# Flamingo-style stack of eight gated layers on one core: the last batch's attention result stays in an SBUF tile

## The reference

```
# layer 0: 16 heads of 32, a second small attention over the last 16 context rows is added
ctx = _attn(q, k, v) + _attn(q, k_dca, v_dca)
x = x + tanh(g_xattn[0]) * (ctx @ Wo + bo)
...
# layer 3: 32 heads of 16, rotary positions
attn = einsum('bhqk,bhkd->bqhd', softmax(q k^T * scale), v)
x = x + tanh(g_xattn[3]) * (attn @ Wout + bout)
# behind it: a mixture of experts, 2 shared and 16 routed, top 2, on _layernorm(x)
```

## Time and profile before

| | us |
|---|---|
| median of 3 runs | 3114.33 (3113.45 to 3116.43) |
| the profiled execution, its own time | 3107.09 |
| its span in the trace | 3105.4 |
| TensorE busy in the span | 2389.4 |
| VectorE busy | 2056.9 |
| ScalarE busy | 1503.2 |
| GpSimd busy | 1075.3 |
| mean granted TensorE clock | 0.906 of full |

### The profile page before, as it was taken

The page is one execution under the profiler, slowest core; times in us unless marked ns, Lnnn a source line. Parts: engine busy times, 40 slices in busy tenths (PEclk is TensorE's granted clock), DMA queues, the critical chain, the costliest instruction groups (busy, mean ns, idle before and its releaser), DMA issues. The chain is left out here.

```text
span 3105.4 us, 39908 instructions
## 1 busy us (share of the span) xinstructions
PE 2389.4 (77%) x13100; PEld 1074.2 (35%) x13100; DVE 2056.9 (66%) x3302; ACT 1503.2 (48%) x2076; POOL 1075.3 (35%) x818
## 2 busy tenths in 40 slices
PE   2989997899969934676666489928898888796882
PEld 0542332344434311222222256614422222353551
DVE  6658774545456798999997652246588888456523
ACT  2554554254332765555553353325557777433642
POOL 4766765011001235666664121155541000001224
PEclk9998999899979967889987599968889999998996
DMA  4542221120000000000000462254522100313735
GB/s 157 179 171 86 86 86 66 63 86 1 1 4 13 1 0 1 0 1 0 0 0 28 136 200 86 82 152 155 209 96 82 61 9 15 103 48 130 247 129 194
DMA packets 128413, 245.60 MB, mean 79 GB/s; under 512 B 32515, under 2 KB 59407, under 8 KB 126310
## 3 DMA queue, kind: packets, MB, share of 16 engines
q1 hardware_dynamic: 107094, 169.49, 15.6%
q0 software_dynamic: 21136, 73.68, 7.7%
HBM read 154.24 MB, written 88.60 MB: 78 GB/s over the span
## 5 line engine op out<-in xcount | busy, mean ns | idle before, releaser
L1901 DVE TENSOR_REDUCE ac_nmax<-ac_M 128x1 f32<-128x512 f32 (+1 forms) x768 | 491.6, 677 | 75.4 <-PE ac_M L1734 70.8
L1883 ACT ACTIVATE ac_PT<-ac_S 128x1024 f32<-128x1024 f32 x384 | 388.0, 1021 | 187.4 <-PE ac_S L1761 168.4
L3477 POOL TENSOR_TENSOR sc_hc<-sc_h,sc_cs 128x1024 f32<-128x1024 f32 x128 | 300.5, 2355 | 157.2 <-DVE sc_h L3592 93.0
L3592 DVE TENSOR_TENSOR_SCAN sc_h<-sc_dA,sc_dB 128x1024 f32<-128x1024 f32 x128 | 292.1, 2282 | 12.3 <-ACT sc_dA L3558 12.3
L3512 PE MATMUL sc_y<-sc_hc,ident 128*128 128x512 f32 x512 | 258.0, 631 | 18.6 <-DVE x_res L3608 16.3
L3558 ACT ACTIVATE sc_dA<-ss_delta,sc_A 128x511 f32<-128x511 f32 x256 | 166.0, 682 | 28.8 <-DVE sc_h L3592 28.0
L774 DVE SCALAR_TENSOR_TENSOR mo_y16l<-mo_yT,mo_y16h 128x512 f16<-128x512 f32 x86 | 59.4, 690 | 180.6 <-ACT mo_y16h L717 180.4
L3490 PE MATMUL sc_b<-ss_bc,sc_sel 128*128 128x512 f16 x128 | 53.5, 418 | 154.1 <-DVE sc_dB L3584 122.7
L3584 DVE TENSOR_TENSOR sc_dB<-ss_du,sc_b 128x1024 f32<-128x1024 f32 x128 | 156.1, 1220 | 17.7 <-PE sc_b L3490 6.9
L3563 ACT ACTIVATE sc_cs<-sc_c 128x512 f32<-128x512 f32 x128 | 76.2, 596 | 185.3 <-POOL sc_hc L3477 182.3
L1734 PE MATMUL ac_M<-KT,QT 64*128 64x512 f16 (+1 forms) x384 | 135.7, 428 | 31.9 <-DVE ac_nmax L1901 17.3
(11 more groups left out here) (622 smaller groups left out, 5716.1 us busy)
## 6 DMA issues: line engine op xcount, KB each, us to landing
keys_t<-ap_kto SPq DMA_DIRECT2D x32, 512.0 KB, 2.6
queries_t<-ap_qto SPq DMA_DIRECT2D x32, 512.0 KB, 2.7
slot_results_last<-mo_o SPq DMA_DIRECT2D x47, 256.0 KB
slot_results<-mo_o SPq DMA_DIRECT2D x39, 256.0 KB
values<-ap_vf SPq DMA_DIRECT2D x32, 256.0 KB, 2.9
ac_KT<-keys_t POOLq DMA_DIRECT2D x4, 2048.0 KB, 8.8
ac_QT<-queries_t POOLq DMA_DIRECT2D x16, 512.0 KB, 10.4
attended<-ac_A SPq DMA_DIRECT2D x8, 1024.0 KB, 3.8
```

The lines of the kernel that those rows point to most:

```text
L1883: nc.scalar.activation(PT[:, n % PTB, :, :], psS[:, 2 * (n % 2):2 * (n % 2) + 2, :], ACT.Exp, scale=SCALE / (SQK * SQK)).then_inc(exp_done, 1)
L1901: last = v.tensor_reduce(out[:, :, 0], sc[:, 0:MAIN], AX.X, ALU.max)
L3477: nc.gpsimd.tensor_tensor(hc[:, m % RC, :, :], h[:, m % RH, :, :], cs[:, m % 2, :].unsqueeze(1).to_broadcast([P, W, S]), ALU.mult).then_in ...
L3592: nc.vector.tensor_tensor_scan(h[:, m % RH, :, :].rearrange("p c s -> p (c s)"), dA[:, m % 2, :, :].rearrange("p c s -> p (c s)"), dB[:, m ...
```

## The change

In both attention layers the last batch's result is written into `Vc` in place of `A`, it is neither stored nor loaded, and the blocks behind the core take the row tiles in the order 12, 13, 14, 15, 0, 1, ..., 11. `Vc` now lives until the end of the layer, where it was freed with the core's tiles. In `attention_output_block` the tile `A` holds three batches. The wait of VectorE for the third batch's store goes too, since the fourth batch has a tile of its own.

```diff
@@ attention_core_block
+        def attended(b):
+            return w["Vc"] if b == B - 1 else A
...
-            sp.wait_ge(whole, B * NG)
-            sp.dma_start(w["a_d"][B - 1], A[:]).then_inc(a_out, 16)
-            sp.wait_ge(a_out, 16 * B)
+            sp.wait_ge(a_out, 16 * (B - 1))
...
-                av = A[:, :, c0:c0 + GH * HD].rearrange("p j (h d) -> p j h d", d=HD)
+                av = attended(G // NG)[:, :, c0:c0 + GH * HD].rearrange("p j (h d) -> p j h d", d=HD)
...
-                if g % NG == 0 and b and i == 0:
+                if g % NG == 0 and 0 < b < B - 1 and i == 0:
                     dve.wait_ge(a_out, 16 * b)
...
@@ attention_output_block
-        A = sb("A", [P, B, TPB, D])
+        A = sb("A", [P, B - 1, TPB, D])
...
+        def attended(t):
+            return w["Vc"][:, t, :] if t < TPB else A[:, t // TPB - 1, t % TPB, :]
+
+        def row_tile(t):
+            return (t + NT - TPB) % NT
...
-            for b in range(B):
+            for b in range(B - 1):
                 sp.dma_start(A[:, b], w["a_d"][b]).then_inc(a_in[b], 16)
...
-                if t % TPB == 0:
-                    pe.wait_ge(a_in[t // TPB], 16)
+                if t and t % TPB == 0:
+                    pe.wait_ge(a_in[t // TPB - 1], 16)
...
@@ late_block
+        def attention(t):
+            return w["Vc"][:, t, :] if t < TPB else A[:, (t - TPB) % NA, :]
...
-            for t in range(NA):
+            for t in range(TPB, TPB + NA):
                 attended(t)
...
             for k in range(NT):
-                if k + NA < NT:
+                if TPB <= k and k + NA < NT:
                     attended(k + NA)
...
-                pe.wait_ge(a_in[t % NA], 16 * (t // NA + 1))
+                if t >= TPB:
+                    pe.wait_ge(a_in[(t - TPB) % NA], 16 * ((t - TPB) // NA + 1))
...
@@ layer_attention
+        w["Vc"] = tile("Vc", [P, TPB, D])
...
-            w["Vc"] = core_tile("Vc", [P, TPB, D])
```

More of the change, by code:

```diff
@@ L1938, in normed @@
                 c0 = g % NG * GH * HD
-                av = A[:, :, c0:c0 + GH * HD].rearrange("p j (h d) -> p j h d", d=HD)
+                av = attended(b)[:, :, c0:c0 + GH * HD].rearrange("p j (h d) -> p j h d", d=HD)
                 spread = rec[:, :, :, i:i + 1].to_broadcast([P, TPB, GH, HD])
@@ L2011, in transposes @@
                 for k in range(KD):
-                    last = nc.tensor.transpose(pt[t % NA][:, k, :], A[:, t // TPB, t % TPB, k * P:(k + 1) * P],
+                    last = nc.tensor.transpose(pt[t % NA][:, k, :], attended(t)[:, k * P:(k + 1) * P],
                                                env.id32[:])
@@ L2050, in _ @@
             dve.wait_ge(x_done, NT)
-            nc.vector.bn_stats(out=env.stats[:, NT - 1, :], in_=env.x[:, NT - 1, :])
+            r = row_tile(NT - 1)
+            nc.vector.bn_stats(out=env.stats[:, r, :], in_=env.x[:, r, :])
 def late_block(nc, env, w, routing):
@@ L2112, in attended @@
             def attended(t):
[L2113 removed]
+                u = t - TPB
+                if u >= NA:
                     sp.wait_ge(at_T, t - NA + 1)
[L2115 removed]
+                sp.dma_start(A[:, u % NA, :], w["a_d"][u // TPB][:, u % TPB, :]).then_inc(a_in[u % NA], 16)
             def row(t):
                 sp.wait_ge(y_ready, t + 1)
[L2119 to L2120 removed]
+                r = row_tile(t)
+                sp.dma_start(rows[r * P:(r + 1) * P, :], y[:, t % NY, :]).then_inc(row_out[t % NY], 16)
+            for t in range(TPB, TPB + NA):
                 attended(t)
@@ L2159, in turned_a @@
                 for k in range(KD):
-                    last = nc.tensor.transpose(pa[:, k, :], A[:, t % NA, k * P:(k + 1) * P], env.id32[:])
+                    last = nc.tensor.transpose(pa[:, k, :], attention(t)[:, k * P:(k + 1) * P], env.id32[:])
                 last.then_inc(at_T, 1)
@@ L2185, in logits @@
                     for k in range(KD):
-                        last = nc.tensor.matmul(p_logit[:, t, :], yy[:, tb % 2, k, j * P:(j + 1) * P], ww[:, k, :],
+                        last = nc.tensor.matmul(p_logit[:, row_tile(t), :], yy[:, tb % 2, k, j * P:(j + 1) * P], ww[:, k, :],
                                                 start=(n == 0), stop=(n == 3 * KD - 1))
@@ L2341, in update @@
                 dve.wait_ge(wo_done, t + 1)
-                v.scalar_tensor_tensor(out=env.x[:, t, :], in0=pw[:], scalar=w["thc"][:], in1=env.x[:, t, :], op0=ALU.mult,
+                r = row_tile(t)
+                v.scalar_tensor_tensor(out=env.x[:, r, :], in0=pw[:], scalar=w["thc"][:], in1=env.x[:, r, :], op0=ALU.mult,
                                        op1=ALU.add).then_inc(x_done, 1)
@@ L2346, in statistics @@
                 dve.wait_ge(x_done, t + 1)
-                c.link(v.bn_stats(out=env.stats[:, t, :], in_=env.x[:, t, :]))
+                c.link(v.bn_stats(out=env.stats[:, t, :], in_=env.x[:, row_tile(t), :]))
                 last = v.bn_aggr(out=agg[:, t, :], in_=env.stats[:, t, :])
@@ L2385, in add_shared @@
                 dve.wait_ge(y_ready, t + 1)
-                v.scalar_tensor_tensor(out=env.x[:, t, :], in0=po[t % 2][:], scalar=cs[:], in1=env.x[:, t, :], op0=ALU.mult,
+                r = row_tile(t)
+                v.scalar_tensor_tensor(out=env.x[:, r, :], in0=po[t % 2][:], scalar=cs[:], in1=env.x[:, r, :], op0=ALU.mult,
                                        op1=ALU.add).then_inc(sh_done, 1)
```

14 lines of the change are left out of this document (9 added, 5 removed).

## The result

| | us |
|---|---|
| changed kernel, median of 4 runs | 3091.02 (3087.63 to 3095.24) |
| kernel before, 4 runs beside them | 3115.37 (3113.45 to 3116.43) |
| ratio, with its 95% interval | 0.9928 (0.9916 to 0.9940) |
| the profiled execution, its own time and span | 3087.63, 3085.9 |

24 us faster, where 15.5 were forecast, and outside the range on the fast side. Some of the distance is the sample. Both kernels were run again on other chips: before at 3112.66 (11 runs), changed at 3090.18 and 3091.05 (5 runs each), so that the effect is nearer to 22 us. There are still 5 to 6 us to be explained.

A forecast was written before the change was run, and what follows sets the result against it. No block was taken as transfer-bound throughout; two HBM round trips of `attended` left all engines idle. Gains of 8.5 and 7.0 us, 15.5 together, took 3114.33 to 3098.8 us, range 3093.5 to 3107.5.

The forecast's parts named there:

- the two gaps: Ends of layer 0's and layer 3's cores: without store and first load, 8.5 and 7.0 us are gained.
- The barrier: Between each core's last instruction and TensorE's first: 0.6 us remains, bounded by 0.42 and 0.73.
- the 1 us that I had named as a sign of being wrong: Both blocks behind the cores: TensorE starting over 1 us after the last arrival would show the prediction wrong.
- Steps and instructions stay as they are. Cost 0: Both blocks behind the cores: the other order of row tiles changes which rows finish first, not how many; cost 0.
- The clock: Starts of both blocks behind the cores: work at low clock costs 3.5 us together, left unchanged by the sum.
- rival 2: Both blocks: low-clock stretches stay as long but lie wholly under TensorE's work; gain 7.9 us, 3106.4; chance 0.12.
- rival 1: Both blocks: shortened gaps keep the clock up, no fall at all; gain 19.0 us, 3095.3; chance 0.17.
- The row at 966 us: Another block end, 963.7 to 966.5: clock stayed full with TensorE mostly idle; cited for rival 1.
- The loads behind: Remaining three loads in each block: they arrive before the fifth row tile needs them; cost 0, in layer 0 at most 1.8 us.
- ScalarE's new wait: Late block: ScalarE waits for the router's weights behind its first `a_high`; costs 0 to 0.4 us, taken as 0.
- rival 3: Block starts: TensorE's instructions come as late as the first load, 4.8 us; gain 7.1 us, 3107.2; chance 0.07.
- The baseline: Whole kernel: the gain is subtracted from 3114.33 us, the median of three runs spanning 3.0 us.

The follow-up runs named there:

- before_fewsem: The kernel before with one semaphore fewer in layer 0's output pass (load batches 2 and 3 share one), nothing else: 3108.37 us, ratio 0.9989.

## Why the prediction was wrong, point by point

The mechanism of the two gaps was right; the sum left out an effect elsewhere in the kernel, which happened to be a gain.

- **The two gaps: right.** Layer 0 gave 9.12 - 1.11 = 8.0 us for 8.5, layer 3 gave 7.61 - 0.32 = 7.3 for 7.0. The barrier, which I took at 0.6 us from a bound of 0.42 to 0.73, is no one number: 1.11 us behind GpSimd and 0.32 behind VectorE, both outside the 0.4 to 0.8 that I expected, and the first beyond the 1 us that I had named as a sign of being wrong. The sum, 15.3 for 15.5, is as close as that because the two errors, 0.5 too much and 0.3 too little, cancel.
- **"Steps and instructions stay as they are. Cost 0": this step failed.** It was said of the two blocks, and I let it stand for the whole kernel. With one semaphore fewer GpSimd's clearing list changed, its loads in layer 3's core came 0.3 us later against VectorE, and a collision in which `rows` had taken 2.67 us came out at 1.12. It brought 3.9 us alone (before_fewsem), and with its 3.2 us in the core it is most of what lies between 15.5 and the 20.6 of the four parts. The row of 2.67 us was in the trace of before, 16 times its usual time, and comparing the longest with the median duration of each line would have shown it. Nothing in that trace says which way it would fall: that it fell on the fast side was luck.
- **The clock: the place was right, the sign was mixed.** I left 3.5 us where they were. In layer 0 rival 2 came true in its mechanism: the stretch moved onto the work and took 2.7 us of the first projection where before it took 1.0 of the transposes; yet pass and feed-forward together came out 0.9 us shorter, since the feed-forward lost most of its second low stretch, which no term of the sum looked at. In layer 3 the low stretch fell from 13.6 and 10.2 us to 3.4, 3.4 and 6.8, and the late block won 1.5 us on average, between nothing and rival 1. No rival happened as a whole. The row at 966 us, where the clock stayed full over 2.8 us with TensorE busy for 0.11, foretold neither place: the clock fell 1.0 us after TensorE had begun again in layer 0, idle for 3.40 us before that (0.8 and 1.2 in the two other profiles), and in layer 3 with TensorE busy for 3.4 of the 6.8 us ahead. What makes it fall, these runs do not show.
- **The loads behind: right.** Cost 0: the three of layer 0 landed in time (4.8 to 8.9 us after their issue, the fifth row tile's transposes 11.2 us after the first), those of the late block too (2.9 to 4.0 us), and ScalarE's new wait of 3.50 us for the router's weights was worth nothing: with the weights first it was 0.60 us, and the block no shorter.
- **The late instruction, rival 3: did not happen.** TensorE started 1.11 and 0.32 us behind the last arrival, where the rival had 4.8.
- **The baseline.** I set the sum against a median of three runs, 3114.33. Later medians of 9 to 21 runs were 3111.8 to 3113.1, so that figure was some 2 us high. That made the prediction too high, by less than what was missed.

## What to carry to other kernels

A round trip that stood alone between two blocks was worth its whole duration here (8.0 and 7.3 us), and could be read off the timeline to half a microsecond: last compute instruction, store, load, first compute instruction. It cost more than that where part of the work behind it ran at half clock (granted 0.50 in the first 3.4 us of layer 0's pass with the stores kept): two stores of 3.5 us cost 11.7, of which the profiles place 3.1 behind the cores. Before costing an edit at its own place only, list what it shifts elsewhere (semaphores, clearing, issue times) and look for instructions whose longest time is many times their median. Here they marked the place where a shift of 0.3 us went with 3.9. The long copy on GpSimd, cut into pieces, shortened every such wait in layer 3's core, from up to 2.67 us to 0.71 at most here.

## What I had not expected of the hardware

- A VectorE instruction on 16 numbers per partition, 0.16 us elsewhere, took up to 2.67 us beside GpSimd: it began while GpSimd issued loads (4.59 us in all) and ended with a copy of 1.90 us that followed at once. Where it came 0.3 us sooner against GpSimd it ended between the two and took 1.12.
- One semaphore fewer in layer 0's output pass, and with it one clearing instruction fewer on GpSimd at 966 us, shifted GpSimd's issue by 0.3 us some 1400 us later, the same in each of nine profiles. With the spread in four pieces the shift was gone (0.56 to 0.57 us in both kernels).
- TensorE busy up to 0.6 us ahead of layer 0's output pass kept the full clock in it (granted 1.00); busy up to 2.7 us ahead did not, and in the late block neither did 1.2. In the changed kernel, with TensorE idle for 3.4 us, it fell as well (0.50). So useless matmuls behind the last real ones, in the changed kernel and in layer 0 alone, look worth 3 us, an estimate from the 3.5 us above. That was not tried.
- The end of the core cost 0.3 us in layer 3, behind VectorE, and 1.1 us in layer 0, behind GpSimd. Whether the engine makes the difference was not tested.
